# Channel attention on one core: sixteen output products in two halves, with a slot of scores between them

## The reference, cut to what matters

```
q = Wq @ target + bq          # (128, 256) for a batch; k and v from the context in the same way
dot = einsum('bhdt,bhds->bhts', q, k) / sqrt(8)      # 16 heads of 8 rows
dot = mask * dot - (1.0 - mask) * 1e6
amap = softmax(dot, axis=-1) * mask
out = einsum('bhts,bhds->bhdt', amap, v)
x = x + tanh(g) * out
```

## Time and profile before

| what | us |
|---|---|
| median of three runs | 1793.42 (1790.8 to 1793.77) |
| span of the profiled execution | 1830.3 |
| PE, DVE, ACT busy over the span | 1720.2, 1141.9, 965.4 |
| stretch from the first W to the W of slot 14 thirteen batches later | 202.74 |
| PE, DVE, ACT busy in that stretch | 197.08, 185.10, 168.02 |

### The profile page before, as it was taken

One profiled execution on the slowest core, in us unless ns is written; L12 is line 12 of the kernel. 1 busy time (PEld: TensorE's weight loads), 2 busy tenths in 40 slices (PEclk: granted clock), 3 DMA queues, 4 the chain that ended last, 5 costly groups with the idle time before them and its releaser, 6 DMA issues. The chain is left out here.

```text
span 1830.3 us, 34413 instructions
## 1 busy us (share of the span) xinstructions
PE 1720.2 (94%) x11824; PEld 1436.8 (78%) x11832; DVE 1141.9 (62%) x2556; ACT 965.4 (53%) x2526; POOL 567.8 (31%) x624
## 2 busy tenths in 40 slices
PE   8999997698999999999999999999999988788988
PEld 6666664458788888888888888888888876677876
DVE  5899988897456556566566555555555668533334
ACT  2688875596455544445455455444454446244433
POOL 3233325534512111112121111111111226556664
PEclk8999997899999999999999999999999998898999
DMA  5011122102100100101001110001000034423337
GB/s 201 14 37 37 37 83 94 58 6 97 50 12 13 47 1 21 40 1 36 24 12 36 35 40 24 13 13 35 1 13 1 1 75 136 123 84 98 110 92 280
DMA packets 48825, 97.45 MB, mean 53 GB/s; under 512 B 7370, under 2 KB 29050, under 8 KB 47668
## 3 DMA queue, kind: packets, MB, share of 16 engines
q1 hardware_dynamic: 40071, 72.57, 12.9%
q0 software_dynamic: 7584, 21.37, 3.9%
q10 hardware_dynamic: 1000, 1.26, 0.2%
HBM read 73.85 MB, written 20.97 MB: 52 GB/s over the span
## 5 line engine op out<-in xcount | busy, mean ns | idle before, releaser
L2288 POOL TENSOR_TENSOR hold_wq<-hold_wq,ca_rsum 128x512 f32<-128x512 f32 x128 | 133.2, 1041 | 794.6 <-DVE ca_rsum L2530 794.6
L2141 ACT ACTIVATE hold_wq<-hold_wq,ca_nb,ca_evens 128x128 f32<-128x128 f32 x256 | 124.2, 486 | 226.9 <-DVE ca_nb L2525 226.9
L2141 ACT ACTIVATE hold_wq<-hold_wq,ca_nb,c_rqs 128x128 f32<-128x128 f32 x256 | 124.2, 486 | 222.2 <-DVE ca_nb L2525 222.2
L1054 DVE TENSOR_REDUCE a_mx<-a_s 128x2 f32<-128x512 f32 x256 | 167.4, 683 | 35.0 <-PE a_s L904 33.5
L797 ACT ACTIVATE a_prob<-a_s 128x512 f32<-128x512 f32 x256 | 148.2, 604 | 62.7 <-PE a_s L924 62.3
L2305 PE MATMUL ca_qk<-early_x,cw_wqkv_h 128*128 128x512 f32 x384 | 162.0, 422 | 1.2 <-PEq L1507 1.2
L2307 PE MATMUL ca_qk<-early_x,cw_wqkv_l 128*128 128x512 f32 x384 | 151.7, 395 | 0.0
L2306 PE MATMUL ca_qk<-early_x,cw_wqkv_h 128*128 128x512 f32 x384 | 151.3, 394 | 0.0
L2426 PE MATMUL ca_acc<-ca_wo_h,ca_oT_h 128*128 128x256 f32 x512 | 145.7, 285 | 0.2 <-DVE ca_oT_l L2539 0.2
L2427 PE MATMUL ca_acc<-ca_wo_l,ca_oT_h 128*128 128x256 f32 x512 | 144.8, 283 | 0.0
L2428 PE MATMUL ca_acc<-ca_wo_h,ca_oT_l 128*128 128x256 f32 x512 | 144.7, 283 | 0.0
(11 more groups left out here) (537 smaller groups left out, 4890.6 us busy)
## 6 DMA issues: line engine op xcount, KB each, us to landing
early_big<-slot_results SPq DMA_DIRECT2D x16, 512.0 KB
mw_raw<-in_d_expert_w SPq DMA_DIRECT2D x12, 352.0 KB, 5.6
a_wraw<-a_heads SPq DMA_DIRECT2D x32, 128.0 KB
a_heads<-a_osb SPq DMA_DIRECT2D x124, 32.0 KB
mw_down<-in_d_expert_d SPq DMA_DIRECT2D x1, 2816.0 KB
token_rows<-early_rows SPq DMA_DIRECT2D x1, 2176.0 KB, 16.1
hold_wk<-in_c_wkT SPq DMA_DIRECT2D x1, 2064.0 KB
hold_wq<-in_c_wqT SPq DMA_DIRECT2D x1, 2064.0 KB
```

The source lines that it names most:

```text
L1054: dve.tensor_reduce(mx[:, b % 2, :, h], s1_bank(b, u)[:, :, :], AX.X, ALU.max)\
L2141: ins = act.activation(prob[:, p, b, :], prob[:, p, b, :], ACT.Exp, bias=nb[:, p, b:b + 1], scale=row_scale[layer][:, r:r + 1], accum_out= ...
L2288: pool.tensor_tensor(prob[:, k % 2, :, :], prob[:, k % 2, :, :], rsum[:, k % 2, :].unsqueeze(2).broadcast_to([P, GB, TOKENS]), ALU.mult)\
```

## The change

`weigh` gets the half as an argument. The first half (`t` = 0) stays in the slot of the block with all its waits, the second half comes one slot later, behind that slot's scores and bias, with no wait of its own. From slot `SLOW` (the last blocks of the stage) both halves stand together one slot later, as the whole block did before. `copied` is one slot later for every batch: slots 4 and 12.

```diff
         def weighed(t):
-            w = t - A_LAG - 3
-            if w >= SLOW:
-                w = w - 1 if w >= SLOW + 1 else -1
-            return (w // U, w % U // A_SLOTS) if 0 <= w < ALL and w % A_SLOTS == A_SLOTS - 1 else None
+
+            halves = []
+            for half in range(2):
+                w = t - A_LAG - (4 if half == 1 or t - A_LAG - 4 >= SLOW else 3)
+                if 0 <= w < ALL and w % A_SLOTS == A_SLOTS - 1 and (half == 1 or w < SLOW or t - A_LAG - 4 == w):
+                    halves.append((w // U, w % U // A_SLOTS, half))
+            return halves
 
         def copied(t):
-            b, rest = divmod(t - A_LAG - (12 if t > ALL + 6 else 11), U)
+            b, rest = divmod(t - A_LAG - 12, U)
...
-                def weigh(b, j):
-                    pe.wait_ge(prob_ready, U * b + A_SLOTS * (j + 1))
+                def weigh(b, j, t):
                     o = out_bank(b, j // 2)
...
-                    for t in range(2):
-                        for v in range(A_SLOTS):
...
-                    mm.then_inc(out_psum, 1)
...
+                    for v in range(A_SLOTS):
...
+                    if t == 1:
+                        mm.then_inc(out_psum, 1)
...
-                    if weighed(t):
-                        weigh(*weighed(t))
+                    for half in weighed(t):
+                        weigh(*half)
```

More of the change, by code:

```diff
@@ new lines, in weigh @@
+                    if t == 0:
+                        pe.wait_ge(prob_ready, U * b + A_SLOTS * (j + 1))
+                        if j == 0:
+                            pe.wait_ge(v_ready, b + 1)
+                        if b == 0 and j == 0:
+                            pe.wait_ge(work.gram_lo, work.grams_to(0))
+                        if j % 2 == 0 and o is proj[0]:
+                            pe.wait_ge(work.gram_lo, work.grams_to(2))
+                        if j % 2 == 0 and o is not out:
+                            pe.wait_ge(k_stack, 2 * BATCHES)
+                            pe.wait_ge(v_ready, BATCHES)
+                        if j % 2 == 0 and o is out:
+                            after(pe, out_copied, 2 * b + j // 2 if b < BATCHES - 1 else 2 * b - 1)
@@ new lines, in weigh @@
+                    for v in range(A_SLOTS):
+                        r = (v + 2) % A_SLOTS
+                        mm = pe.matmul(o[A_ROWS * r:A_ROWS * r + A_ROWS, j % 2, :],
+                                       vT[:, b % A_BUFS, t, A_TILES * r + j, :],
+                                       prob[:, (U * b + A_SLOTS * j + v) % PR, t, :], start=(t == 0), stop=(t == 1),
+                                       skip_group_check=True)
+                    if t == 1:
+                        mm.then_inc(out_psum, 1)
```

## The result

The changed kernel took 1802.02 us (median of 20 runs, 1791.69 to 1821.72) against 1795.7 for the kernel before (20 runs, 1787.7 to 1798.68). The ratio is 1.0047, 95% interval 1.0031 to 1.0064, so it is some 8.4 us slower (1795.7 x 0.0047; 5.6 to 11.5 by the interval). The medians lie only 6.3 us apart; the ratio isn't taken from them, and it leaves out the run of 1821.72 us as a slow one. The span of the profiled execution is 1800.7 us.

A forecast was written before the change was run, and what follows sets the result against it. No engine alone bounds it; TensorE's work and waits make a 15.58 us batch. Waits of 1.26 go, work of 1.36 comes: 15.68, +1.3 over 13 batches, +0.1 past them, 1793.4 + 1.4 = 1794.8 us; range 1789 to 1803.

The forecast's parts named there:

- no change: The outcome as laid out: the waits move but the change pays as much as it takes out, 1792 to 1797 us.
- rival 2: In slots 0, 8 and 12 the bias doesn't run beside its slot: 0.66 for 0.44 us, 1803.4 total; chance 0.15.
- The prices of the pieces: On TensorE: half of W 0.57 us, lone slot 0.43, slot with bias 0.44; splitting adds 0.34 a block.
- Rivals 1 and 2: The first: splitting is cheaper, a half's drain overlaps the next scores; 1788.5 us, chance 0.20. The second: see rival 2.
- A rule weighed: The skill page's drain figure would price a split block at 0.11 us in place of 0.34, making a gain.
- The waits in slots 5 and 6 and in slot 11: Slots 5 and 6 lose their 0.80 us wait; slot 11's second scores wait 0.21 for the exponential of slot 9.
- W6 and the copy: W6 starts 2.10 us after slot 4 starts, with a 0.32 wait because the later copy is late for the bank.
- The clock column is at 1.00 ... so no clock term enters: The profiled stretch of thirteen batches runs at 2.4 GHz all through, so the clock adds nothing to the sum.
- The near ties: Five places in a batch, slot 8 on the maxima's DMAs among them, where data comes barely in time; no wait counted.
- rival 3: Each of the five near ties comes 0.05 us late in the mean: +0.25 a batch, 1798.0 us; chance 0.15.
- The tail past the stretch: Behind the thirteen batches, four second halves cost 0.14 us each and one falling behind slot 255 costs -0.43: sum +0.1.

The follow-up runs named there:

- e6: The change, with W6 waiting for the copy alone and the exponential of slot 4 for its scores alone; a profile only, one time 1800.96 us.
- e1: The change with halves and later copy only from slot 80 on, earlier blocks whole; ratio 1.0020 to the kernel before, 1797.4 us.
- e7: The kernel before (whole blocks) with the later copy, mask in slot 6 and one DMA for the maxima; ratio 0.9984, 1791.86 us.
- e8: The change with mask in slot 6 and one DMA for the maxima; ratio 1.0029 to the kernel before, 1798.33 us.
- e2: The change with halves and later copy only up to slot 79; ratio 1.0025 to the kernel before, 1797.67 us.
- e4: The change with the mask two slots later, in slot 6; ratio 1.0038 to the kernel before, 1800.3 us.
- e5: e2 with the first half's matmuls issued twice in the split blocks, output unchanged; ratio 1.0024 to the kernel before, 1799.24 us.
- e3: The kernel before (whole blocks) with only the copy and its mask moved to slots 4 and 12; ratio 1.0013.

## Why the prediction was wrong

The time lay in the range and the direction of the sum was right (+1.4 us), but I called it no change with 0.50 and it is slower by 8.4 us. That it lies in the range is luck: the range reached up to 1803 for rival 2, which the trace refutes. Point by point:

- *The prices of the pieces* held: halves 0.57 forecast, lone slots 0.43, slot with bias 0.44; the trace has the same to 0.01. Rivals 1 and 2 fall by it, and so does the estimate of 0.11 us for a split block ("A rule weighed"): it costs 0.34 us of TensorE.
- *The waits in slots 5 and 6 and in slot 11* went and came as forecast (0.44 and 0.20).
- *W6 and the copy*: the term was mis-sized. It was 2.10 us from S4 and 0.32 of wait; the trace has 2.26 and 0.47. e6 shows that the 0.15 comes from second waits on two instructions, to which the sum gave nothing. That makes a batch 15.83, not 15.68: 13 x 0.25 = 3.3 us in place of 1.3. e1 agrees: ten batches, 2.5 to 2.9 us expected, 0.20% (3.6 us; 0.5 to 6.5) measured.
- *"The clock column is at 1.00 ... so no clock term enters"* is the step that failed. I read the clock of one trace from the first W on and put its term at nothing. The clock falls in the slots ahead of it: at 41 us in the trace of before, where it is back before the first W, at about 59 us in others, and in e7 and e8 not at all. Where it fell at 59 us it stayed low for 14 us with whole blocks (e1), 24 in the change and in e2, 65 in e4, and 14 again with the first half doubled (e5). In e6, the change with fewer waits, it fell twice, at 40 us for 10 and at 64 us for 20. e2 sets the term apart: 0.25% for three batches whose length accounts for 0.04%, some 3.8 us, though its interval is wide; its trace has the stage 6.1 us longer.
- *The near ties* (rival 3) broke nowhere in the trace of the change; the maxima's DMAs held slot 8 only where W6 came earlier (e3, e4, and one batch of e6). The tail past the stretch didn't matter, as forecast: from the stretch's last W (268.22 before, 277.21 now) to the last maxima it is 23.0 us in both traces.

So the loss is about 3.3 us of longer batches and about 4 us of time at 1.2 GHz (an estimate: the 24 us against the 14 of e1, by the 0.40 of e4); the two make 7 to 7.5 of the 8.4 us, inside the interval of 5.6 to 11.5. Whether the remainder is real I can't tell: compared at a mean clock of 0.978 to 0.979 alone, the change is 5.5 us above before (7 and 26 runs), where the batches give 3.3.

Why the clock comes back later is only narrowed down, and stays open. The runs point to the split blocks between slots 30 and 79 (e1 against e2), not to the later copy (e3 has it, and no run with a low mean clock) and not to the number of changes of shape alone (e5). The stretches at 1.2 GHz were seen in one trace of each kernel, and where the clock falls differs between them; that whole blocks bring it back sooner after a fall at 59 us rests on one trace, e1. The count of low mean clocks is what supports it.

## What to carry to other kernels

Breaking a block up to fill waits pays its own filling and emptying at every new edge, and here that was more (1.36 us a batch) than the waits it took out (1.79 - 0.67 = 1.12). When a periodic schedule is priced piece by piece, look for all loops of nearly the same length, in the old order too: shortening one (e3) gave nothing until the second went, and then a third held. A clock that stands at full level in a stretch of one trace isn't fixed: look for its nearest fall, here 15 us ahead of the stretch, at what runs just before and just after it, and ask what the change does there.

## What the runs showed of the hardware

- A second semaphore wait on an instruction that stalls cost time: 0.16 us over an instruction of ACT and one of TensorE that hangs on it (e6, 2.10 against 2.26).
- The same small transfer as one DMA in place of four takes 0.56 us of issue on SP in e7, where the four took 2.44.
- Score matmuls and a bias in different row groups ran together: a slot with its bias, three groups, took 0.44 us in the change, a slot alone, two groups, 0.43 to 0.44.
- Where the granted clock fell to 1.2 GHz at about 59 us, ahead of the first W, it stayed there for 14 us with whole blocks (e1) and for 24 us (the change, e2) or 65 us (e4) with split ones, one trace each.
